# A two-layer gated cross-attention stack: layer 0 scores of eight heads per visit, their products in the common PSUM ring, low query parts on GpSimd, and a new order of steps

## The reference

```python
x = x + tanh(g_xattn[0]) * cross_attention_0(ln(x), ctx)      # 16 heads of 64
x = x + tanh(g_ffn[0])   * soft_mixture_0(ln(x))              # 8 experts, threshold 0.1
x = x + tanh(g_xattn[1]) * cross_attention_1(ln(x), ctx)      # 16 heads of 16
x = x + tanh(g_ffn[1])   * routed_experts_1(ln(x)[:512])      # the first two batches' tokens
```

## Time and profile before

| | us |
|---|---|
| median of 3 runs (3987.91 to 3991.95) | 3990.4 |
| the profiled execution | 3989.64 |
| its span, first to last instruction | 3987.9 |

### The profile page before, as it was taken

One profiled execution on the slowest core, in us unless ns is written; L12 is line 12 of the kernel. 1 busy time (PEld: TensorE's weight loads), 2 busy tenths in 40 slices (PEclk: granted clock), 3 DMA queues, 4 the chain that ended last, 5 costly groups with the idle time before them and its releaser, 6 DMA issues.

```text
span 3987.9 us, 90593 instructions
## 1 busy us (share of the span) xinstructions
PE 3868.0 (97%) x30740; PEld 3196.4 (80%) x30740; DVE 2946.5 (74%) x6752; ACT 2068.6 (52%) x3881; POOL 1065.3 (27%) x1301
## 2 busy tenths in 40 slices
PE   5999999999999999999999999999999999999959
PEld 4788888888888888888888888888888888888845
DVE  3777777777777777777777777777777777777756
ACT  4555555555555555555555555555555555555521
POOL 2223222322323322322332232332232233223210
PEclk9999999999999999999999999999999999999979
DMA  2000000000000000000000000000000000000001
GB/s 87 14 16 9 15 14 9 15 14 9 15 14 13 12 15 14 9 15 14 9 15 14 9 15 14 10 15 15 14 9 15 14 9 15 14 9 15 11 28 53
DMA packets 57906, 64.79 MB, mean 16 GB/s; under 512 B 5232, under 2 KB 54672, under 8 KB 57104
## 3 DMA queue, kind: packets, MB, share of 16 engines
q10 hardware_dynamic: 34688, 32.52, 2.6%
q1 hardware_dynamic: 23184, 31.81, 2.3%
HBM read 47.01 MB, written 17.30 MB: 16 GB/s over the span
## 4 chain that ended last, share of the span: by engine, by line
PE 92%; ACT 3%; issue 2%; DVE 2%; DMA 1%; POOL 0%; DVEq 0%; SPq 0%; POOLq 0%; ACTq 0%
PE g L647 29%; PE g L653 16%; PE scores L647 12%; PE scores L789 12%; PE scores L743 6%; PE g L798 3%; PE scores L772 3%; PE g L667 2%; ACT prob L576 2%; PE g L710 2%; PE scores L747 1%; PE g L721 1%; PE g L728 1%; PE g L677 1%; PE scores L776 1%
## 5 line engine op out<-in xcount | busy, mean ns | idle before, releaser
L576 ACT ACTIVATE prob<-scores 120x1024 f32<-120x1024 f32 x512 | 510.6, 1023 | 478.7 <-PE scores L747 329.4
L1112 DVE SCALAR_TENSOR_TENSOR x<-g,lg_w,x 128x256 f32<-128x256 f32 x1024 | 494.7, 483 | 195.4 <-PE g L647 173.1
L456 POOL TENSOR_TENSOR q_lo<-an,q_hi 128x256 fp32r<-128x256 f32 x512 | 369.2, 732 | 772.6 <-ACT q_hi L607 772.6
L789 PE MATMUL scores<-prob,vx 120*128 120x256 f32 x2048 | 548.0, 390 | 3.8 <-DVE an L1007 2.7
L1007 DVE TENSOR_TENSOR an<-scores,inv 64x256 f32<-64x256 f32 x1024 | 423.6, 414 | 126.7 <-ACT inv L597 118.9
L647 PE MATMUL g<-ew_hi,yT_hi 128*128 128x512 f32 x1024 | 462.8, 452 | 0.0
L595 ACT ACTIVATE inv<-scores 64x512 f32<-64x512 f32 x512 | 304.1, 594 | 296.5 <-PE scores L789 288.2
L1051 DVE TENSOR_REDUCE y_nm<-g 128x4 f32<-128x480 f32 x512 | 300.9, 650 | 184.4 <-PE g L721 184.4
L789 PEld LDWEIGHTS scores<-prob,vx 120*128 120x128 f32 x2048 | 358.3, 190 | 70.3 <-ACT prob L576 2.8
L647 PE MATMUL g<-ew_lo,yT_hi 128*128 128x512 f32 x1024 | 405.0, 396 | 0.0
L647 PE MATMUL g<-ew_hi,yT_lo 128*128 128x512 f32 x1024 | 403.4, 394 | 0.0
(11 more groups left out here) (208 smaller groups left out, 9355.0 us busy)
## 6 DMA issues: line engine op xcount, KB each, us to landing
x_in<-in_x ACTq DMA_DIRECT2D x64, 256.0 KB, 2.7
out<-y_x SPq DMA_DIRECT2D x64, 256.0 KB, 2.1
ctx_in<-in_ctx ACTq DMA_DIRECT2D x128, 120.0 KB, 2.2
wk_s<-in_gu SPq DMA_DIRECT2D x8, 512.0 KB, 3.9
wk_s<-in_wq SPq DMA_DIRECT2D x1, 1024.0 KB, 4.8
wv_s<-in_wo SPq DMA_DIRECT2D x1, 1024.0 KB, 4.8
wk_s<-in_ew SPq DMA_DIRECT2D x1, 1024.0 KB, 5.1
wv_s<-in_ew SPq DMA_DIRECT2D x1, 1024.0 KB, 4.9
```

The lines of the kernel that those rows point to most:

```text
L456: g.tensor_tensor(q[1][:, p, :], an[:, p % 3, :], q[0][:, p, :].bitcast(F32), ALU.subtract).then_inc(x_attn_lo.sem, 1)
L576: a.activation(prob[:, e % 2].rearrange("p o u s -> p (o u s)"), scores[0:NK, banks, :].rearrange("p o c -> p (o c)"), ACT.Exp, scale=scal ...
L789: ins = t_.matmul(pv[p % 2][:, o * S:(o + 1) * S], vx[0:NK, 2 * p + o, :], prob[:, p // 2 % 2, o, p % 2, :], start=True, stop=True)
L1112: ins = v.scalar_tensor_tensor(out=x1[:, t, :], in0=ring.bank(Y_FFN[j])[:, o * D:(o + 1) * D], scalar=lg_w[:, t, 2 * n + o:2 * n + o + 1], ...
```

## The change

- x_st 0 and 1 each compute two quads, one into scores banks 0 and 1, the other into banks 2 and 3, and each has two exponentials. Four visits a batch become two.
- x_pv and z_out are jobs of the ring; x_out uses scores bank 0. The semaphores for them become the ring's.
- n_q: ScalarE copies the whole bank to q_full after the high part, which empties the bank; GpSimd subtracts the high part from the copy (256 instructions in all). VectorE's part is gone. The copy waits for GpSimd's subtraction two n_q before; x_st waits for the subtraction of its quad.
- ORDER is new; 59 jobs in the ring where 50 were.

```diff
 
 
 ORDER = (
-    ("x_st", 0), ("y_k", 0), ("z_hi", 1), ("y_ffn", 0), ("y_v", 0), ("n_load", 0), ("z_out", 0), ("n_stat", 0),
-    ("x_pv", 0), ("x_mul", 0), ("y_ffn", 1), ("n_norm", 0), ("y_ffn", 2), ("x_st", 1), ("x_pv", 1), ("x_mul", 1),
-    ("n_tr", 0), ("x_st", 2), ("x_pv", 2), ("y_ffn", 3), ("y_ffn", 4), ("x_mul", 2), ("x_hi", 0), ("x_hi", 1),
-    ("x_pv", 3), ("x_mul", 3), ("y_ffn", 5), ("x_pv", 4), ("y_ffn", 6), ("n_ctx", 0), ("x_hi", 2), ("y_ffn", 7),
-    ("y_stat3", 0), ("x_mul", 4), ("x_st", 3), ("x_hi", 3), ("x_pv", 5), ("y_norm3", 0), ("x_mul", 5), ("p_load", 0),
-    ("n_k", 0), ("x_hi", 4), ("x_pv", 6), ("y_tr3", 0), ("n_k", 1), ("x_hi", 5), ("x_mul", 6), ("x_pv", 7),
-    ("x_mul", 7), ("y_q", 0), ("x_hi", 6), ("x_hi", 7), ("n_v", 0), ("y_res", 0), ("x_out", 0), ("y_max", 0),
-    ("x_out", 1), ("x_out", 2), ("y_max", 1), ("x_out", 3), ("p_stat", 0), ("y_maxt", 0), ("n_q", 0), ("n_q", 1),
-    ("p_norm", 0), ("n_q", 2), ("y_maxt", 1), ("n_q", 3), ("p_tr2", 0), ("n_max", 0), ("y_st", 0), ("n_max", 1),
-    ("p_gate", 0), ("n_max", 2), ("n_maxt", 0), ("p_lg", 0), ("y_st", 1), ("y_mul", 0), ("y_pv", 0), ("n_v", 1),
-    ("n_max", 3), ("p_wt", 0), ("y_pv", 1), ("n_maxt", 1), ("p_ctx", 0), ("p_eb", 0), ("y_mul", 1), ("n_res", 0),
-    ("y_hi", 0),
+    ("y_ffn", 0), ("n_load", 0), ("y_ffn", 1), ("x_st", 0), ("y_k", 0), ("n_stat", 0), ("x_pv", 0), ("x_pv", 1),
+    ("x_mul", 0), ("z_hi", 1), ("x_mul", 1), ("x_hi", 0), ("x_hi", 1), ("y_ffn", 2), ("x_st", 1), ("x_pv", 2),
+    ("x_pv", 3), ("n_norm", 0), ("y_ffn", 3), ("x_mul", 2), ("x_mul", 3), ("y_ffn", 4), ("y_ffn", 5), ("y_ffn", 6),
+    ("x_hi", 2), ("y_ffn", 7), ("y_stat3", 0), ("y_v", 0), ("n_tr", 0), ("n_ctx", 0), ("x_pv", 4), ("y_norm3", 0),
+    ("x_pv", 5), ("x_mul", 4), ("x_hi", 3), ("x_mul", 5), ("n_k", 0), ("x_hi", 4), ("y_tr3", 0), ("x_pv", 6),
+    ("x_pv", 7), ("x_hi", 5), ("x_mul", 6), ("x_mul", 7), ("z_out", 0), ("x_hi", 6), ("p_load", 0), ("y_q", 0),
+    ("x_hi", 7), ("n_k", 1), ("x_out", 0), ("y_max", 0), ("x_out", 1), ("y_res", 0), ("x_out", 2), ("y_max", 1),
+    ("x_out", 3), ("p_stat", 0), ("y_maxt", 0), ("n_q", 0), ("n_q", 1), ("p_norm", 0), ("y_maxt", 1), ("n_q", 2),
+    ("n_q", 3), ("n_max", 0), ("p_tr2", 0), ("y_st", 0), ("n_max", 1), ("n_res", 0), ("p_gate", 0), ("n_max", 2),
+    ("n_v", 0), ("p_lg", 0), ("n_maxt", 0), ("y_mul", 0), ("y_st", 1), ("y_pv", 0), ("n_max", 3), ("p_wt", 0),
+    ("y_hi", 0), ("n_v", 1), ("y_pv", 1), ("n_maxt", 1), ("y_mul", 1), ("p_ctx", 0), ("p_eb", 0),
 )
 AHEAD = {"n": 1, "x": 0, "p": 0, "y": -1, "z": -2}
 FILLS = ("n_ctx", "n_tr", "n_k", "n_v", "n_q", "n_max", "n_maxt", "p_tr2", "p_gate", "p_lg", "p_ctx", "p_wt", "p_eb",
-         "y_pv", "y_k", "y_v", "y_ffn", "y_tr3", "y_q", "y_max", "y_maxt")
+         "x_pv", "z_out", "y_pv", "y_k", "y_v", "y_ffn", "y_tr3", "y_q", "y_max", "y_maxt")
 NG = 4
 
 
...
-Y_PV = [("y_pv", m) for m in range(KD)]
+X_PV, Y_PV, Y_OUT = [("x_pv", p) for p in range(NPAIR)], [("y_pv", m) for m in range(KD)], ("z_out", 0)
...
-        q = pair("q", [P, NPAIR, S])
+        q, q_full = pair("q", [P, NPAIR, S]), sb("q_full", [P, 2, 2 * S])
...
+        x_kmx, x_qlo = signal("x_kmx", 2), signal("x_qlo", 4)
+        x_scored, x_probs = signal("x_scored", QUADS), signal("x_probs", QUADS)
...
-                y_made.wait(sp, i, 1)
+                ring.empty(sp, i, Y_OUT)
                 sp.dma_start(out_rows[i], y_x3[:]).then_inc(y_stored.sem, 16)
...
+            def x_q(i, c):
+                ring.empty(pool, i, X_Q[c])
+                g.tensor_tensor(flat(q[1][:, 2 * c:2 * c + 2, :]), q_full[:, c % 2, :],
+                                flat(q[0][:, 2 * c:2 * c + 2, :]).bitcast(F32), ALU.subtract).then_inc(x_qlo.sem, 1)
...
-                       "n_k": x_k, "x_hi": x_lo})
+                       "n_k": x_k, "n_q": x_q, "x_hi": x_lo})
...
             def x_q(i, c):
                 hi_of(x_hi, i, X_Q[c], 2 * S, flat(q[0][:, 2 * c:2 * c + 2, :]))
+                x_qlo.wait(act, i, c - 1)
+                ring.has_emptied(a.copy(q_full[:, c % 2, :], ring.bank(X_Q[c])[:, 0:2 * S]), X_Q[c])
...
             def x_st(i, g):
-                x_scored.wait(act, i, g + 1)
-                if g >= 2:
-                    x_mixed.wait(act, i, 2 * g - 2)
-                exp(g, slice(0, 2), SCALE0, x_probs)
+                for e in (2 * g, 2 * g + 1):
+                    x_scored.wait(act, i, e + 1)
+                    if e >= 2:
+                        ring.full(act, i, X_PV[2 * e - 3])
+                    exp(e, slice(e % 2 * 2, e % 2 * 2 + 2), SCALE0, x_probs)
...
             def x_pv(i, p):
-                x_mixed.wait(act, i, p + 1)
+                ring.full(act, i, X_PV[p])
                 if p >= 2:
-                    x_attn.wait(act, i, p - 1)
-                invert(pv[p % 2][64:128, :], inv[:, p % 2, :], x_logged, x_recip, i, p + 1)
+                    ring.empty(act, i, X_PV[p - 2])
+                invert(ring.bank(X_PV[p])[64:128, :], inv[:, p % 2, :], x_logged, x_recip, i, p + 1)
 
             def x_attn_split(i, p):
-                x_attn.wait(act, i, p + 1)
+                ring.empty(act, i, X_PV[p])
                 a.copy(q[0][:, p, :], an[:, p % 3, :]).then_inc(x_attn_hi.sem, 1)
...
+                at = g % 2 * 2
...
-                            t_.matmul(scores[0:NK, o, cols], keys(rows, p)[a], queries(rows, p)[b],
...
             def x_st(i, g):
                 ring.all_empty(pe, i, X_MAXT)
-                if g >= 1:
-                    x_probs.wait(pe, i, g)
-                scores_of_quad(g, lambda rows, p: both(kT, rows, p, ALL),
-                               lambda rows, p: both(q, rows, p, ALL), x_nmT).then_inc(x_scored.sem, 1)
+                for e in (2 * g, 2 * g + 1):
+                    x_qlo.wait(pe, i, e + 1)
+                    if g >= 1:
+                        x_probs.wait(pe, i, e - 1)
+                    scores_of_quad(e, lambda rows, p: both(kT, rows, p, ALL),
+                                   lambda rows, p: both(q, rows, p, ALL), x_nmT).then_inc(x_scored.sem, 1)
 
             def y_st(i, m):
                 ring.all_empty(pe, i, Y_MAXT)
                 if m == 0:
-                    y_made.wait(pe, i, 0)
...
             def x_pv(i, p):
                 x_probs.wait(pe, i, p // 2 + 1)
-                if p == 0:
-                    ring.all_empty(pe, i, X_V)
-                if p >= 2:
-                    x_attn.wait(pe, i, p - 1)
-                elif p == 1:
-                    y_made.wait(pe, i - 1, 0)
+                ring.to_fill(pe, i, X_PV[p], *(X_V if p == 0 else ()))
                 for o in range(2):
-                    ins = t_.matmul(pv[p % 2][:, o * S:(o + 1) * S], vx[0:NK, 2 * p + o, :], prob[:, p // 2 % 2, o, p % 2, :],
+                    ins = t_.matmul(ring.bank(X_PV[p])[:, o * S:(o + 1) * S], vx[0:NK, 2 * p + o, :], prob[:, p // 2 % 2, o, p % 2, :],
                                     start=True, stop=True)
-                ins.then_inc(x_mixed.sem, 1)
+                ring.has_filled(ins, X_PV[p])
...
-                    x_attn.wait(pe, i, NPAIR)
                 x_attn_lo.wait(pe, i, k0 + 4)
-                ins = products(pv[0][:, t * D:(t + 1) * D],
+                ins = products(scores[:, 0, t * D:(t + 1) * D],
...
+                ring.to_fill(pe, i, Y_OUT)
                 for t in range(T):
-                    ins = products(pv[1][:, t * D:(t + 1) * D],
+                    ins = products(ring.bank(Y_OUT)[:, t * D:(t + 1) * D],
                                    [(both(q1, ALL, k, slice(t * P, (t + 1) * P)),
                                      (w1o_s(0)[:, k, :], w1o_s(1)[:, k, :])) for k in range(KD)])
-                ins.then_inc(y_out_in.sem, 1)
+                ring.has_filled(ins, Y_OUT)
...
             def x_mul(i, p):
                 x_recip.wait(dve, i, p + 1)
+                if p < 2:
+                    y_attn_lo.wait(dve, i - 2, p + 1)
                 if p >= 3:
                     x_attn_lo.wait(dve, i, p - 2)
-                normalised(pv[p % 2], p % 2, an[:, p % 3, :]).then_inc(x_attn.sem, 1)
+                ring.has_emptied(normalised(ring.bank(X_PV[p]), p % 2, an[:, p % 3, :]), X_PV[p])
...
-
-            def x_q(i, c):
-                lo_of(x_hi, 4 + c, i, X_Q[c], 2 * S, flat(q[1][:, 2 * c:2 * c + 2, :]),
-                      flat(q[0][:, 2 * c:2 * c + 2, :]))
...
-                    v.scalar_tensor_tensor(out=flat(x1[:]), in0=pv[0], scalar=tg[:, 0:1], in1=flat(x_res[:]),
+                    v.scalar_tensor_tensor(out=flat(x1[:]), in0=scores[:, 0, :], scalar=tg[:, 0:1], in1=flat(x_res[:]),
...
+                ring.full(dve, i, Y_OUT)
+                ring.has_emptied(v.scalar_tensor_tensor(out=flat(y_x3[:]), in0=ring.bank(Y_OUT)[:], scalar=tg[:, 1:2],
+                                                        in1=flat(y_x3[:]), op0=ALU.mult, op1=ALU.add), Y_OUT)
```

(24 more changed lines are left out.)

## The result

The changed kernel takes 3970.6 us (median of 5; 3969.8 to 3972.4) where the kernel before took 3990.4 (3987.9 to 3992.5): a ratio of 0.995, interval 0.9937 to 0.9964. Forecast was 3995, "no change"; the range of 3948 to 4035 holds the time. So the likeliest case was wrong: the time went the other way by 20 us.

The account below looks back on a forecast made before the run. TensorE, busy 97%, was taken as the bound. Per batch, - 0.78 + 0.80 + 0.05 + (1.13 - 1.05) = + 0.15 us; + 0.08 was taken, 5 us in all, giving 3995 us, range 3948 to 4035.

Parts of the forecast that it names:

- the credit for the waits of before: TensorE's waits between x_out and the next x_st in the old order, 1.05 us a batch, subtracted from the new waits.
- The stall at p_tr2: TensorE waits 0.5 us a batch at p_tr2 because GpSimd's low parts hold p_norm on VectorE; bounds 0 and 0.75.
- 0.05 at y_max 0: y_max 0 finds its bank 0.05 us late, since n_k 1's low part now comes right before it.
- setup and the last layer's tail are untouched: Outside the repeated batch periods, before the first and after the last, the forecast put no change in time.
- Scores of two quads a visit: Layer 0 scores (x_st): two visits fewer a batch, each costing 0.39 us to enter and leave, save 0.78 us.
- The wait at y_ffn 5: TensorE waits 0.8 us a batch for the bank x_mul 2 frees, late through the exponential behind x_pv 3.
- the wake-up: A TensorE wait after its queue ran dry costs 0.3 us beyond the time until its release.
- ScalarE is late: Rival: the exponential behind x_pv 3 overruns its 0.4 us slack; 4014 to 4033 us, chance 0.16.
- The low query parts: Subtractions move from VectorE to GpSimd, about 1.33 us each; two in a row hold p_norm, stalling p_tr2 0.5 us.
- p_norm is held once: Rival: one GpSimd operation only holds p_norm, 0.3 us a batch less, 3976 us; chance 0.16.
- keeps the port over all four: Rival: GpSimd holds p_norm through all four low parts, 2.6 us more a batch, 4160 us; chance 0.04.
- The other new waits: New-order TensorE waits per batch: n_max 2 and n_v 0 together 0.15 us, n_v 1 0.3, y_ffn 0 0.18.

Follow-up runs that it names:

- the first experiment: The kernel after with the layer 0 scores back to four visits of one quad, all else kept: 4017.0 us, ratio 1.0066 against the kernel before.
- the two that paid: The kernel after with exponential 3 behind the inversions, x_mul 2 ahead of y_ffn 3, and low query parts 0 and 1 on VectorE: 3902.6 us, ratio 0.9782 against before.

## Why the prediction was wrong, by its steps

The mechanisms forecast are there; the step that failed is a term of the sum, the credit for the waits of before. It was read as 1.05 us a batch and measures 1.25. The stall at p_tr2 was 0.12 smaller than forecast, and 0.05 at y_max 0 did not come; the three together turn the + 0.15 into a minus. Outside the periods, "setup and the last layer's tail are untouched" failed too.

**Scores of two quads a visit: right.** - 0.78 forecast, - 0.77 in the account, and the first experiment gives the same 0.39 a visit in the other direction. The Trainium skill's page "TensorEngine Tiling (Array Packing)", section "Key Properties", states that changing the tiling mode drains TensorE; the trace agrees in that switching has a price for these 64-row matmuls between full ones, 0.19 us on entering and 0.20 on leaving.

**The wait at y_ffn 5: right, in size and cause.** 0.80 forecast, 0.76 measured; the 0.3 for the wake-up from the earlier trace rows fits (0.55 from the end of x_mul 2 to the end of the first matmul, of which a matmul in a stream would take 0.23). ScalarE was free for exponential 3 in time: it sat idle 0.50 us before it, released by the last product of x_pv 3, so the rival "ScalarE is late" is out. The slack was 0.50 where 0.4 had been worked out.

**The low query parts: right in mechanism, the stall 0.12 too large.** GpSimd held VectorE twice in a row, p_norm ended at x_out + 6.3 (6.5 forecast), and p_tr2 waited 0.38 (0.5). The rival "p_norm is held once", whose 3976 lies nearest to the measured time, is refuted by the pair of 2.69 us: its number came close for another reason. The rival "keeps the port over all four" would have put the pair beyond 5 us; it is out too.

**The other new waits: right but for tenths.** n_max 2 and n_v 0 together about 0.2 (0.15 forecast), n_v 1 0.26 (0.3), y_ffn 0 0.26 (0.18), y_max 0 none (0.05).

**The waits of before in the stretch: the term that failed within the period.** The forecast credited 1.05 us. In the account the products of that stretch (n_maxt, p_gate, n_max, p_ctx, p_lg, n_v, y_pv 1) cost 0.79 less in all, after paying the new 0.46; so the waits that went were 1.25. The same 40 periods, split by job, show where the missing 0.20 stood (us a batch):

```
waits of before                          read   measured
n_max 0                                  0.06   0.05
p_gate, n_max 2 and n_maxt 0             0.71   0.75   (0.18, 0.35 and 0.23, rounded)
p_lg                                     0.05   0.03
y_pv 1                                   0      0.08
n_maxt 1                                 0.13   0.22
p_ctx                                    0.10   0.12
sum                                      1.05   1.25
```

y_pv 1 and n_maxt 1 carry 0.17 of it. The first stood where the walk looked for no small waits. At n_maxt 1 one batch showed 0.44 where the mean is 0.48, and 0.31 was taken for its length without a wait where the kernel after shows 0.26.

The corrected sum, beside the one on record:

```
term                                   forecast   measured
two visits fewer                        -0.78      -0.77
y_ffn 5 and y_ffn 0                     +0.98      +1.00
y_max 0                                 +0.05       0
p_tr2                                   +0.50      +0.38
rest of the stretch, new less old       -0.60      -0.79
sum a batch                             +0.15      -0.18 (periods: -0.16)
```

Three terms between 0.05 and 0.2 lean the same way. The sum was a difference of two large numbers, 2.0 us added and 1.8 taken away, so 0.2 in either decides its sign, and a batch counts 63 times: from the + 0.08 taken to the - 0.163 measured is 15 us.

**"Setup and the last layer's tail are untouched": wrong, by 7 us.** The first x1 comes 3.4 us sooner. Two things changed on the way to it, the clock and the order. Windows of TensorE in before and then in after (window and its length, busy us and instructions, granted clock as a share of 2.4 GHz, DMA share, GB/s):

```profile
50.00:55.00 5.00, 3.51 (x27) 1.00 0.00 0
55.00:60.00 5.00, 3.58 (x10) 0.64 0.01 3
60.00:65.00 5.00, 3.71 (x21) 0.50 0.00 0
65.00:70.00 5.00, 3.88 (x22) 0.50 0.24 77
```

```profile
50.00:55.00 5.00, 4.05 (x34) 1.00 0.00 0
55.00:60.00 5.00, 3.84 (x15) 1.00 0.01 3
60.00:65.00 5.00, 4.09 (x40) 1.00 0.24 77
...
70.00:75.00 5.00, 1.52 (x7) 0.85 0.01 2
75.00:80.00 5.00, 5.00 (x28) 0.81 0.02 5
```

Before, the clock was at 1.2 GHz from 56.4 to 70.0 us, and 10.4 us of TensorE's work fell into that stretch; after, it was at 1.2 GHz from 73.5 to 76.9, with 3.2 us of work. One matmul of n_v adds 0.85 us in that stretch and 0.43 at 2.4 GHz, so the lower clock cost half of it, 5.2 us of busy time before and 1.6 after. From 36 us to the first x1 TensorE was busy 48.7 us before and 43.5 after, 5.2 less. The clock accounts for 3.6 of that. The rest is work put off and not saved, 1.7 us: n_v 0 of the second batch, four matmuls of 0.43, stood ahead of the first x1 in the old order and stands behind it in the new one. Against the 5.2 stand 1.8 us more of idle time (11.3 for 9.5), which leaves the 3.4.

What the clock alone was worth is not shown; its cost in busy time need not reach the first x1. In three of the kernels with the new order (GpSimd's subtractions behind p_norm, x_mul 2 ahead of y_ffn 3 alone, and the two that paid) the stretch at 1.2 GHz ahead of the first x1 is 6.8 us long, twice that of the kernel after, and the first x1 comes at 91.1, 90.6 and 90.7 us, against 90.8. Nor do these rows settle what let the clock fall: the same three were busy 3.5 of 5 us from 50 to 55, as before, and 4.3 or 4.4 in the next 5, and kept 2.4 GHz until 71 to 72 us. In all ten kernels with the new order the first x1 comes at 89.8 to 91.8 us, the 91.8 being the one with four visits; there is one trace of before.

From the last x1 to the end, TensorE is as busy as before (134.4 us for 134.6) at the same clock (0.83 for 0.82), and its waits are shorter. Its waits for `xn` there, of before and then of after:

```profile
PE g L667 <- DVE xn L966: 8.4, 2, 5.1
```

```profile
PE g L672 <- DVE xn L967: 6.6, 2, 3.3
```

That is - 1.8. The wait for `yT_lo` (1.5), that for `turned` (0.9) and 0.4 of the loading wait for `wv_s` are gone too, and 1.0 comes back at y_pv: - 3.4 with small ones, which with the 0.2 less of busy time is the whole difference. Without layer 0 beside it, the order of layer 1's own steps decides, and it is a different one; which of its moves matters was not tried. The walk of one batch in the steady state could show none of this.

**The chances.** Faster had 0.33, and the forecast's own spread put 0.03 below 3982. With terms this small against steps of 0.05 in the walk, that spread was too narrow: the difference within the periods came from the forecast case with its sizes off, not from a rival.
